# Applying the edge types to two batches at once in the 24-target rounds of a graph network kernel

## What is computed

```python
h = relu(node_features @ node_proj_w.T + node_proj_b)
for l in range(2):
    trans = einsum('nh,tdh->tnd', h, edge_W[l])      # 8 types
    msgs  = trans[edge_type, src]
    agg   = segment_sum(msgs, dst, num_segments=num_nodes)
    h = relu(gru_cell(agg, h, ...))
return x + h @ out_w.T + out_b
```

## Time and profile before

| What | us |
|---|---|
| median of 3 runs | 2214.71 (2210.90 to 2219.23) |
| the profiled execution, its own time | 2202.64 |
| its span, first to last instruction | 2200.8 |
| ten wide rounds of layer 0 (863.54 to 1160.60) | 297.06 |
| ten wide rounds of layer 1 (1902.70 to 2170.51) | 267.81 |
| mean granted TensorE clock over the span | 0.852 |

### The profile page before, as it was taken

One profiled execution on the slowest core, in us unless ns is written; L12 is line 12 of the kernel. 1 busy time (PEld: TensorE's weight loads), 2 busy tenths in 40 slices (PEclk: granted clock), 3 DMA queues, 4 the chain that ended last, 5 costly groups with the idle time before them and its releaser, 6 DMA issues.

```text
span 2200.8 us, 34111 instructions
## 1 busy us (share of the span) xinstructions
PE 1611.3 (73%) x10492; PEld 1122.7 (51%) x10493; DVE 809.0 (37%) x3350; ACT 530.0 (24%) x1270; POOL 1191.4 (54%) x1282
## 2 busy tenths in 40 slices
PE   6478787777778756776766688788778775677777
PEld 4345555544444534555554455455445444555565
DVE  6564252424223243444335122221423223434443
ACT  5132232415133112222212011110413311222221
POOL 6455555555555555445542555556555555555552
PEclk9689888999889878877777888998889888888897
DMA  6325436263542322222222666674233252222221
GB/s 171 110 58 161 157 104 210 76 213 93 162 156 71 110 62 68 63 59 63 66 65 65 205 213 225 216 256 128 82 95 111 73 156 74 68 69 68 63 68 38
DMA packets 183315, 251.55 MB, mean 114 GB/s; under 512 B 24396, under 2 KB 156641, under 8 KB 183201
## 3 DMA queue, kind: packets, MB, share of 16 engines
q0 software_dynamic: 58176, 119.22, 19.5%
q1 hardware_dynamic: 123041, 130.73, 18.4%
q10 hardware_dynamic: 1984, 0.13, 0.1%
HBM read 211.87 MB, written 38.12 MB: 114 GB/s over the span
## 4 chain that ended last, share of the span: by engine, by line
PE 37%; another core or an unknown queue 29%; issue 12%; DVE 11%; ACT 3%; DMA 3%; DVEq 3%; POOL 1%; SPq 0%; PEld 0%; ACTq 0%; POOLq 0%; PEldq 0%
PE ps L1053 10%; PE ps L1124 8%; PE ps L1030 7%; PE ps L1116 5%; PE ps L991 3%; PE ps L1104 3%; DMA blocks<-node_table 2%; DVE onehot L1559 2%; DVE acc L1636 2%; ACT counts L767 1%; ACT sums_sb L833 1%; DVEq L1629 1%; DVE acc L1656 1%; DVE work L1516 1%
## 5 line engine op out<-in xcount | busy, mean ns | idle before, releaser
L595 POOL DMA_INDIRECT gath<-node_table,gidx x1212 | 1155.3, 953 | 966.8 <-ACT gidx L633 541.1
L1053 PE MATMUL ps<-counts,blocks 128*128 128x504 f16 (+3 forms) x1764 | 420.3, 385 | 77.4 <-issue 45.2
L1656 DVE TENSOR_TENSOR acc<-ps,acc 128x16 f32 x864 | 150.5, 174 | 872.0 <-PE ps L1124 400.3
L1124 PE MATMUL ps<-sums_sb,wT 128*128 128x128 f32 x1728 | 268.3, 320 | 106.7 <-ACT sums_sb L833 90.1
L833 ACT COPY sums_sb<-ps 128x512 f32<-128x512 f32 x216 | 126.7, 587 | 872.9 <-remote 552.1
L1124 PEld LDWEIGHTS ps<-sums_sb,wT 128*128 128x128 f32 x1728 | 255.6, 232 | 124.7 <-issue 63.2
L1030 PE MATMUL ps<-work 128*128 128x392 bf16 x983 | 226.5, 362 | 118.4 <-issue 46.2
L1053 PEld LDWEIGHTS ps<-counts,blocks 128*128 128x128 bf16 x1764 | 172.0, 101 | 274.4 <-issue 90.2
L1104 PE MATMUL ps<-sums_sb,wT 128*128 128x96 f32 (+1 forms) x1408 | 222.8, 313 | 90.9 <-issue 52.0
L1104 PEld LDWEIGHTS ps<-sums_sb,wT 128*128 128x128 f32 x1408 | 208.0, 226 | 119.6 <-issue 88.8
L1116 PE MATMUL ps<-onehot,gath 128*128 128x128 bf16 x2592 | 203.2, 231 | 52.3 <-issue 29.0
(11 more groups left out here) (200 smaller groups left out, 887.1 us busy)
## 6 DMA issues: line engine op xcount, KB each, us to landing
blocks<-node_table SPq DMA_DIRECT2D x84, 672.0 KB
kept_counts<-counts SPq DMA_DIRECT2D x28, 882.0 KB
counts<-kept_counts SPq DMA_DIRECT2D x28, 882.0 KB
gath<-node_table,gidx POOLq DMA_INDIRECT x1212
node_table<-gath SPq DMA_DIRECT2D x14, 336.0 KB, 3.1
node_table<-work SPq DMA_DIRECT2D x14, 336.0 KB
counts<-in_x_dram SPq DMA_DIRECT2D x1, 3080.0 KB
out_dram<-counts SPq DMA_DIRECT2D x13, 224.0 KB
```

The lines of the kernel that those rows point to most:

```text
L595: nc.gpsimd.indirect_dma_start(out=gath[:, b, j, :], out_offset=None, in_=tables[l], in_offset=bass.IndirectOffsetOnAxis(ap=gidx[:, b, j:j ...
L1053: last = nc.tensor.matmul(head_ps[:, 0:COLS[share]], blocks[:, j % 2, at, part * H:(part + 1) * H], counts[:, a, 0:COLS[share]], start=(i ...
L1124: last = nc.tensor.matmul(narrow_ps[q].rearrange("p (g w) -> p g w", g=2 * BG), wT[:, W_EDGE + l * T + t, :], n_sb[:, q, :, t * NARROW:(t ...
L1656: nc.vector.tensor_tensor(win, narrow_ps[q][:, g * NARROW:(g + 1) * NARROW], win, ALU.add) \
```

## The change

The wide rounds 38 to 47 get the order of the narrow ones. `by_type` stays for the last round. The new `wide_types` applies one type matrix to two batches, 8 x 24 = 192 columns, so that a round has 2 x 8 products in place of 4 x 8; `add_wide` adds eight windows after each. `s_sb` gets four slots. To make room, `typT` is kept in bf16, and `base_row` and `start_row` share one tensor, on partitions 0 and 32. `n_sb` and the early uses of `sums_sb` keep their contents at new places.

```diff
-        base_row = sb("base_row", [1, GROUPS])
-        start_row = sb("start_row", [1, GROUPS], I32)
+        group_rows = sb("group_rows", [33, GROUPS])
+        base_row, start_row = group_rows[0:1, :], group_rows[32:33, :].bitcast(I32)
...
-        win_ps = [ps[:, 4 + b, 0:BG * WIN] for b in range(2)]
+        win_ps = [ps[:, 4 + q, 0:2 * BG * WIN] for q in range(2)]
...
+                def copy_sums(k, b):
+                    act.wait_ge(es[l]["win_done"], k + b // 2 * 2)
+                    act.copy(s_sb[:, b // 2, b % 2 * BG:(b % 2 + 1) * BG].rearrange("p (a g) c -> p a g c", a=2),
+                             sums[b % 2]).then_inc(es[l]["sums_copied"], 1)
...
+                def wide_types(k, q):
+                    pe.wait_ge(es[l]["sums_copied"], k + (2 * q + 4))
+                    pe.wait_ge(es[l]["acc_added"], (k + 2) * BG)
+                    for t in range(T):
+                        last = nc.tensor.matmul(win_ps[q].rearrange("p (g w) -> p g w", g=2 * BG),
+                                                wT[:, W_EDGE + l * T + t, :],
+                                                s_sb[:, q, :, t * WIN:(t + 1) * WIN],
+                                                start=(t == 0), stop=(t == T - 1))
+                    last.then_inc(es[l]["win_done"], 2)
...
                     sum_by_code(k, landed, 0)
                     sum_by_code(k, landed, 1)
                     piece(pe, begin, gates_begin, k, tile)
-                    by_type(k, 0)
+                    sum_by_code(k, landed, 2)
                     piece(pe, begin, gate_in, l + 1, tile)
-                    sum_by_code(k, landed, 2)
-                    by_type(k, 1)
+                    wide_types(k, 0)
                     piece(pe, begin, gate_z, l + 1, tile)
                     sum_by_code(k, landed, 3)
-                    by_type(k, 2)
-                    by_type(k, 3)
+                    wide_types(k, 1)
                     piece(pe, begin, to_rows, l + 1, tile)
...
-                    for b in range(SLOTS):
-                        g0 = n * ROUND + b * BG
-                        add_windows(k, g0, b)
-                        one_hots(g0 + ROUND, b)
-                        if b == 0:
+                    for q in range(2):
+                        if q == 0:
                             piece(dve, begin, before_tanh, l + 1, tile)
-                        elif b == 1:
+                        add_wide(k, n * ROUND + 2 * q * BG, q)
+                        for b in (2 * q, 2 * q + 1):
+                            one_hots(n * ROUND + (ROUND + b * BG), b)
+                        if q == 0:
                             piece(dve, begin, new_state, l + 1, tile)
-                        elif b == 3:
+                        else:
                             piece(dve, begin, state_parts, l + 1, tile)
```

More of the change, by code:

```diff
@@ L240, in gnn_kernel @@
         relT = sb("relT", [GE, GROUPS + AHEAD])
-        typT = sb("typT", [GE, GROUPS + AHEAD])
+        typT = sb("typT", [GE, GROUPS + AHEAD], BF16)
         code = sb("code", [GE, GROUPS + AHEAD])
@@ L311, in gnn_kernel @@
         hots = onehot.rearrange("p b g c -> p (b g c)").bitcast(F32)
-        places = (one_half[0:ROWP, 0, 0:RC * GE], one_half[0:ROWP, 1, 0:RC * GE], hots[0:ROWP, 0:RC * GE])
+        places = (one_half[0:ROWP, 0:RC * GE], one_half[0:ROWP, RC * GE:2 * RC * GE], hots[0:ROWP, 0:RC * GE])
         dst_i, src_i, typ_i = (rows(t, I32) for t in places)
@@ L798, in one_round @@
                         act.wait_ge(es[l]["sums_ready"], k + (b + 1 + SLOTS))
-                        act.wait_ge(es[l]["win_done"], k + (b + 1))
-                        act.copy(s_sb[:, b % 2].rearrange("p (a g) c -> p a g c", a=2), sums[b % 2]) \
-                           .then_inc(es[l]["sums_copied"], 1)
+                        copy_sums(k, b)
                         update(b, n, begin, tile)
@@ L808, in last_round @@
                         act.wait_ge(es[l]["sums_ready"], k + (b + 1 + SLOTS))
-                        act.wait_ge(es[l]["win_done"], k + (b + 1))
                         if b < SLOTS - 1:
-                            act.copy(s_sb[:, b % 2].rearrange("p (a g) c -> p a g c", a=2), sums[b % 2]) \
-                               .then_inc(es[l]["sums_copied"], 1)
-                        else:
-                            act.copy(s_sb[:, b % 2, 0:LAST_GROUPS], sums[b % 2][:, 0, 0:LAST_GROUPS]) \
+                            copy_sums(k, b)
+                        else:
+                            act.wait_ge(es[l]["win_done"], k + 2)
+                            act.copy(s_sb[:, 1, BG:BG + LAST_GROUPS], sums[1][:, 0, 0:LAST_GROUPS]) \
                                .then_inc(es[l]["sums_copied"], 1)
@@ L1102, in by_type @@
                     pe.wait_ge(es[l]["acc_added"], (k + (b + 1)) * BG)
+                    at = b % 2 * BG
                     for t in range(T):
@@ L1637, in add_windows, with add_wide @@
                           .then_inc(sem_l["acc_added"], 1)
+                def add_wide(k, g0, q):
+                    for half in range(2):
+                        _, starts = nc.values_load_multi_w_load_instructions(
+                            start_row[0:1, ds(g0 + half * BG, BG)], engines=(mybir.EngineType.DVE,), min_val=0, max_val=N,
+                            skip_runtime_bounds_check_because="start_row is clamped to N, and nodes are not negative")
+                        if half == 0:
+                            dve.wait_ge(sem_l["win_done"], k + (2 * q + 4))
+                        for j in range(BG):
+                            g = half * BG + j
+                            win = acc[:, ds(starts[j], WIN)]
+                            dve.wait_ge(sem_l["acc_added"], k * BG + ((2 * q + 2) * BG + g))
+                            nc.vector.tensor_tensor(win, win_ps[q][:, g * WIN:(g + 1) * WIN], win, ALU.add) \
+                              .then_inc(sem_l["acc_added"], 1)
                 def add_narrow(k, g0, q, after_head, hots):
```

8 lines of the change are left out of this document (4 added, 4 removed).

## The result

| What | before, us | after, us |
|---|---|---|
| median of 4 runs | 2213.63 (2210.90 to 2219.23) | 2235.08 (2229.66 to 2243.94) |
| the profiled execution, its own time | 2202.64 | 2229.66 |
| ten wide rounds of layer 0 | 297.06 | 302.06 |
| ten wide rounds of layer 1 | 267.81 | 286.40 |
| everything else of the span | 1635.9 | 1639.4 |

What follows compares the result with a forecast made beforehand. No engine is full in the wide rounds; streams of gathers halt TensorE, ScalarE and VectorE until they end. Layer 0's +15 and layer 1's +21 us make +36 on the median 2214.7: 2251 us, range 2200 to 2275.

Steps and rivals of the forecast that it cites:

- layer 1: Wide rounds of layer 1: two streams of eight gathers become one of twelve; 28.9 against 26.8 us, +21 us for ten.
- layer 0: Wide rounds of layer 0: 32.0 us a round against 30.5, +1.5 each, +15 us for ten.
- First half: Wide round from copy 0 to copy 3: released by its twelve gathers, 19.1 us.
- The step that costed 16 fewer records in the stream at nothing: First half: taking 16 products off TensorE's list gains 0, hidden by the 15 us that twelve gathers take.
- the gate and copy 3 are let go together: End of the first half: the halt ends with the stream of gathers, releasing ScalarE's gate, with copy 3 right after.
- Second types: Types of batches 2 and 3 after copy 3: 16 records of 192 columns at 1.2 GHz, 5.4 us, 1.6 more than narrow.
- The second half of layer 0: From copy 3 to the next copy 0: the narrow round's 10.6 us plus 2.2, so 12.8 us.
- First types: First types of a wide round, inside the stream of gathers: about 2.7 us.
- B: Rival: TensorE at 2.4 GHz for the second types, 2.8 us, VectorE never waits; -21 us, 2194; chance 0.15.
- C: Rival, no change: first half shortens or layer 1 keeps two streams of eight, balancing a loss; +5 us, 2220; chance 0.15.
- D: Rival: TensorE's instructions are slow to come, 0.6 us each in the halt; up to 130, say -80 us, 2135; chance 0.05.
- E: Rival: halt moves to a worse place, 16 gathers in one stream, rounds 33 to 34 us; +95 us, 2310; chance 0.05.

Runs made afterwards that it cites:

- the kernel of 96 columns: The changed kernel's order, with two products of 96 columns per type in place of one of 192: 2315.3 us with halts, ratio 1.035; 1.0151 without.
- The second pair by batch: The changed kernel with types 2 and 3 again in separate products of 96 columns, first pair kept wide: 2209.16 us with halts, ratio 1.0011; 1.0064 without.
- the split: The changed kernel with batch 2's gathers asked for only after sums 3, giving two streams of eight: 2217.75 us with halts, ratio 0.9908; 1.0091 and 1.0077 without.

## Why the prediction came out as it did

**Direction right, layer 1 right, layer 0 three times too large.** The sum was +15 in layer 0 and +21 in layer 1; measured were +5.0 and +18.6. The whole was +36 and the medians differ by 22. Part of the 15 is a mixed measure: layer 0's forecast was held against a typical round of 30.5 us, layer 1's against the mean of 26.8, though layer 0's mean was 29.7.

**First half: right in size, incomplete in cause.** 19.1 us forecast, 18.8 measured in layer 0 and 19.9 in layer 1, with twelve gathers in a row in both. The step that costed 16 fewer records in the stream at nothing was too strict: they are worth 1.2 us at copy 3 in layer 0, by the kernel of 96 columns, and 0.3 in layer 1. The value of 19.1 held most of the 1.2 all the same, since it was read from narrow rounds, which have as few records. What was wrong in part is that the gate and copy 3 are let go together, when the stream ends: copy 3 is, but in layer 0 the gate came 1.6 to 3.7 us ahead of it in seven of the ten rounds, and in the round shown VectorE's adds, from 10.4 us after copy 0 on, were done amid the stream. That the stream's length sets this half on a chip with halts is shown by the stream of eight: 14.3 us. That a stream makes a halt wherever it runs is not: on the other chips the same gathers run sixteen and more in a row with no halt. What differs between the chips stays open.

**Second types: the right term, too large in layer 0.** Forecast 5.4 us at the lower clock, measured 4.4 to 5.4 in layer 0 (4.54 to 4.57 in four of ten) and 4.7 to 5.5 in layer 1. Where the lower level held to the end the forecast was right: the types at 1984.82 in layer 1 took 5.49 us at a granted clock of 0.50. In layer 0 the clock rose on the way, 0.50 up to 943.0 and 0.97 from there to the end of the types at 944.1; the stretch from copy 3 to the fifth add shows both levels in its mean:

```profile
938.74:944.37 5.63, 4.78 (x20) 4.76 (x21) 3.15 (x7) 1.46 (x3) 3.15 (x3) 0.62 0.12 35
```

In the narrow round of the earlier trace rows the 3.78 us of the types passed at 0.50 and the stretch behind them, 829 to 833, at 0.89: its types end before the rise, and longer ones run into it. VectorE waited 2.2 us (2.5 forecast). The second half of layer 0 was 11.9 us where 12.8 was forecast. Of the 10 us by which layer 0 came out better than the sum, this is one half: nine rounds grew by 0.9 us each in place of 1.5. The other half is the tenth round, which I had treated like the rest: it got 3.2 us shorter (25.4 to 22.2).

**First types: right.** 2.76 us, forecast 2.7. The Trainium skill's page "TensorE: Matmul & The Clock Gate" (Part 3, on packing small matmuls) says in its list of what overlaps that weight loads overlap products in flight only across row groups; the same part also names a background weight buffer as a way to overlap. 96 columns cost 1.95 us for 16 records, 0.12 each, and 192 columns 2.76, 0.17 each. 448 columns take 0.375 (two in 0.75 us from one start to the next, in the same round), so 192 alone would take 0.16, and 16 of them 2.6 us. So at 192 columns it is the columns that set the pace, and the weights are nearly wholly hidden; one behind the other they would make 4.5 us. The trace does not bear the rule of that list out for these products.

**Layer 1: right number, half of its reason.** I put the loss down to the merged stream and the lower clock together. The second pair by batch brings the typical round back to 26.5 us with the stream still merged, and the split brings it to 26.0 with the wide types kept. Either alone is enough, so the two don't add up as terms of a sum: the loss comes when a long first half is followed by late work. In the undisturbed rounds the first half was 19.9 us where 19.1 was taken, and the second 9.6 where 9.5 follows from the terms.

**The rivals.** B (clock up, 2.8 us) did not come with halts. Without halts its condition did: in the round of the changed kernel from 727.61 the second types took 2.87 us and VectorE went on to its fifth add without waiting, and still the ratio was 1.0076, because there the gathers fill the round. C did not come: layer 1 lost its two streams. D holds in part: on a chip with halts 16 records more in the stream delayed the gate by 3.1 us and VectorE's adds by 8.7, but copy 3, which asks for the next gathers, by 1.2 only. It is a price for who waits on those results, and most of it doesn't reach the end of the round. Its upper bound of 130 us doesn't follow from what it names: 9.6 us in layer 0 and the 6.8 us down to 20 in layer 1 make 164, which changes neither its value nor its chance. E came in one round out of twenty: at 981.4 fifteen gathers ran in one stream and the round took 32.5 us.

## What to carry to other kernels

The wider product as such was a gain: in the same order it gave 1.0098 with halts where narrow ones gave 1.035. What cost time was to hold a pair's products back until the later batch's sums were there. So leave apart the pair on which another engine waits: here first pair wide, second pair by batch was 0.9% better than both wide (1.0011 against 1.0098, each against the kernel before on its own chip). But it was no faster than the kernel before there, and 0.6% slower on a chip without halts, so joining the first pair has earned nothing in the whole time, though its wide stretches were 17 us shorter in the one execution profiled with halts. Where a stream of gathers holds up the engines, try breaking it at the point from which the next step can run; with halts this took the change from 1.0098 to 0.9908, again on two chips, and without halts it gave nothing, so such an edit has to be measured on both kinds.

## What the runs showed of the hardware that I had not expected

The same kernel takes 2206 to 2236 us (medians) on some chips and 1635 to 1639 on others. Gathers are issued 1.25 us apart on both. With halts, records on TensorE and one-hots on VectorE that follow one another without a pause elsewhere come at multiples of about 0.7 us. In the round of the changed kernel shown above VectorE's one-hots start at 934.37, 935.76, 936.47, 937.87 and 938.62; in the kernel before, types 2 of the round of the earlier trace rows are recorded in pieces:

```profile
1084.48 0.33 PE L1104 MATMUL ps<-sums_sb,wT 128*128 128x96 f32 x1 [0.50 <-ACT sums_sb L800]
1085.88 0.45 PE L1104 MATMUL ps<-sums_sb,wT 128*128 128x96 f32 x2 [1.08 <-issue]
1087.99 0.65 PE L1104 MATMUL ps<-sums_sb,wT 128*128 128x96 f32 x3 [1.67 <-issue]
1089.39 0.32 PE L1104 MATMUL ps<-sums_sb,wT 128*128 128x96 f32 x1 [0.75 <-issue]
```

The granted clock over the span tells the two kinds of chip apart as well, 0.84 to 0.85 in the profiled executions with halts and 0.94 to 0.96 in those without. In the round of the earlier trace rows and in the one shown after, data moved on the queues of gathers and stores alone, so no loading of instructions is seen in the halts; what makes them stays open.
